# Preamble reordered, fc2's bias added by transfers, the last chunks' fc2 cut in pieces (one Trainium2 core)

## The chip, the cores and the metric

The kernel runs on one core of one Trainium2 chip. The metric is device microseconds (us) of one execution. In the profile the engines are PE (TensorE, matmuls; PEld its weight loads), DVE (VectorE), ACT (ScalarE), POOL (GpSimd) and SP (SyncE, which only issues transfers here).

## The reference

Two layers follow each other on x of 2 sequences x 2048 steps x 256 features, all in float32 (`s` is a sigmoid):

```
xn = layernorm(x)                        # no scale, no shift
i, f, o, z = split(xn @ W + b)           # W is 256 x 1024
i = 10*tanh((i + input_bias)/10);  f = -softplus(f);  o = s(o);  z = tanh(z)
step:  m' = max(f + m, i);  c' = exp(f+m-m')*c + exp(i-m')*z
       n' = exp(f+m-m')*n + exp(i-m');      h = o * c' / (n' + 1e-6)
x = x + h / rms(h) * scale
g = layernorm(x) * gamma + beta
y = silu(g @ w1 + b1)                    # w1 = (fc1_q - 128) * fc1_scales, 256 x 1024
x = x + 0.5 * (y @ w2 + b2)              # w2 = (fc2_q - 128) * fc2_scales, 1024 x 256
```

## The kernel before

The 4096 rows are cut into 8 chunks of 512 steps, taken in turn from the two sequences; chunk c follows chunk c-2 in its sequence. Features lie on the 128 partitions for the gates, the recurrence and fc1, time lies on them for the norms and for fc2's result, so each chunk is turned three times on PE: x after the first norm (`x_turned`), h (`h_turned`), and g after the second norm (`g_turned`). Every matrix product is done on split numbers: a high part in fp32r and the rest as a low part, three matmuls for one (hi*hi, hi*lo, lo*hi). So every activation (xt, gt, y) has an ACT copy to its `_hi` and a DVE subtraction to its `_lo`. The recurrence is three scans on DVE (maximum, denominators, numerators), and the division is exp(-ln(n)) on ACT (`reciprocal`) with a Newton step on DVE (`newton`, `refined`).

The kernel is written engine by engine: each engine has its own program, in an order written out by hand, and semaphores tie them together. An engine takes its instructions strictly in that order, so one that waits holds up all that are behind it. From chunk 4 on a loop over t puts in one turn: gates of chunk t, fc2 of chunk t-3, turns of g(t-2), x(t+1) and h(t-1), and fc1 of chunk t-2. After t = 6 the last chunks are written out.

PSUM holds four banks `mm_ps` (gates and fc1), two banks `z_ps` (fc2's sums, half u of a chunk in one bank, tile n = 2u or 2u+1 in half a bank) and two banks `t_ps` (turns). `fc2(c, tiles)` makes tile n of chunk c from 24 matmuls (8 blocks k of y, three passes each), `fc2_both(c, half)` makes the tiles 0 and 2 (half 0) or 1 and 3 (half 1) side by side, block by block, as y arrives. `final(c, u)` on DVE adds half of fc2's sums to the rows and frees the bank for chunk c+1; SP then stores the rows.

What the change touches by name: `base(c)` on POOL turns the rows into what x + layernorm(x) needs with the small scale (four instructions of 128x256); `base_bias(c)` on DVE adds half of b2 to them; `rms_root`, `ln1_root`, `ln2_root` on POOL are the powers -1/2; `ln1_sums`, `ln1_means` and `ln2_sums`, `ln2` on DVE are the statistics; `g_normalised` is on ACT or POOL by chunk; `silu` on ACT makes y and y_hi, `silu_alone` y only, and then DVE makes y_hi (`y_high`) before y_lo (`y_low`). fc1's two scale groups are folded as a `unit` for the bias and activation, a `ratio` that scales w1's second half, and a `share` that is 1 or 0 and scales its first; `spread` turns such a column into rows on PE with 8 transposes.

## Time and profile before

| what | value |
|---|---|
| time, median of 3 runs | 310.02 us (309.99 to 310.45) |
| the profiled execution's own time | 311.77 us |
| its span, first to last instruction | 310.0 us |
| PE busy, matmuls and weight loads | 294.7 us (95%), 256.3 us (83%) |
| DVE, ACT, POOL busy | 269.5 (87%), 229.7 (74%), 126.4 us (41%) |
| mean granted clock of TensorE | 0.988 of full |
| moved by DMA | 14.73 MB, mean 48 GB/s |

A matmul's row in the timeline has its start, its modelled duration and its operands; matmuls overlap, so the work rate is read from start to start, not from durations. Text in square brackets is the idle time of that engine just before the instruction, with what ended it.

### The profile page before, as it was taken

Reading aid. Unit: us, or ns where it says so; the run is one execution under the profiler, and the core shown is the slowest. Engines: PE = TensorE matmul, PEld = TensorE weight load, DVE = VectorE, ACT = ScalarE, POOL = GpSimd, SP = SyncE. Lnnn points to the kernel's source line nnn. Section 1 sums busy time; section 2 is a strip of 40 time slices with the busy share of each in tenths; the row PEclk is TensorE's granted clock in tenths of the full one; section 3 lists DMA queues with packets and bytes.
Section 4 is the critical chain, followed back from the end, with each engine's and each line's share of the span. In section 5 each row is a group of like instructions: output and inputs, shape, how many; then the busy total and the mean of one; then the engine's idle time right before and its main releaser. Section 6 shows DMA issues by size and latency. Waiting matters only on the chain.

```text
span 310.0 us, 4767 instructions
## 1 busy us (share of the span) xinstructions
PE 294.7 (95%) x1728; PEld 256.3 (83%) x1728; DVE 269.5 (87%) x487; ACT 229.7 (74%) x370; POOL 126.4 (41%) x131
## 2 busy tenths in 40 slices
PE   7999999979899899999999999999999799988996
PEld 5778789856897789988897889987898699868896
DVE  3998989999899999999999997999999987692741
ACT  2699987889879966899876978599866983921720
POOL 3043058300290529512970179012992198155000
PEclk9999999899999999999999999999999979999999
DMA  7980021060000030012000300020000011000201
...
DMA packets 11127, 14.73 MB, mean 48 GB/s; under 512 B 720, under 2 KB 10208, under 8 KB 10848
## 3 DMA queue, kind: packets, MB, share of 16 engines
...
q0 software_dynamic: 320, 1.58, 2.6%
...
## 4 chain that ended last, share of the span: by engine, by line
PE 39%; DVE 38%; issue 11%; ACT 5%; POOL 5%; DMA 2%; DVEq 0%; POOLq 0%; ACTq 0%
PE z_ps L236 5%; PE z_ps L237 4%; PE z_ps L238 4%; DVE y_lo L854 4%; PE mm_ps L236 4%; PE mm_ps L237 4%; PE mm_ps L238 4%; DVE rec L763 3%; DVE rec L756 3%; DVE rec L778 3%; DVE g L822 3%; DVE bn L835 3%; PE mm_ps L329 2%; PE mm_ps L322 2%; DVE rows L830 2%
## 5 line engine op out<-in xcount | busy, mean ns | idle before, releaser
L236 PE MATMUL z_ps<-w_hi,y_hi 128*128 128x256 f32 x248 | 71.8, 290 | 2.6 <-DVE rows L891 1.9
L237 PE MATMUL z_ps<-w_lo,y_hi 128*128 128x256 f32 x248 | 70.9, 286 | 0.0
L238 PE MATMUL z_ps<-w_hi,y_lo 128*128 128x256 f32 x248 | 70.8, 286 | 0.0
L573 ACT ACTIVATE y<-mm_ps,b_all,unit 128x512 f32<-128x512 f32 x54 | 41.6, 770 | 12.8 <-PE mm_ps L329 12.8
L236 PEld LDWEIGHTS z_ps<-w_hi,y_hi 128*128 128x128 f32 x248 | 47.6, 192 | 3.8 <-DVE rows L891 2.1
L237 PEld LDWEIGHTS z_ps<-w_lo,y_hi 128*128 128x128 f32 x248 | 47.6, 192 | 0.3
L238 PEld LDWEIGHTS z_ps<-w_hi,y_lo 128*128 128x128 f32 x248 | 47.6, 192 | 0.0
L322 PE MATMUL mm_ps<-gt_hi,w_hi 128*128 128x512 f32 x124 | 39.9, 403 | 1.6 <-ACT y L573 1.6
L854 DVE TENSOR_TENSOR y_lo<-y,y_hi 128x512 fp32r<-128x512 f32 x56 | 37.6, 687 | 4.0 <-ACT y_hi L576 3.7
L236 PE MATMUL mm_ps<-xt_hi,wg_hi 128*128 128x512 f32 x96 | 38.4, 400 | 1.1 <-ACT f_gate L505 1.1
L329 PE MATMUL mm_ps<-gt_lo,w_hi 128*128 128x512 f32 x124 | 38.8, 394 | 0.0
L237 PE MATMUL mm_ps<-xt_lo,wg_hi 128*128 128x512 f32 x96 | 37.9, 395 | 0.0
L238 PE MATMUL mm_ps<-xt_hi,wg_lo 128*128 128x512 f32 x96 | 37.8, 394 | 0.0
L576 ACT ACTIVATE y_hi<-y 128x512 fp32r<-128x512 f32 x54 | 34.2, 633 | 1.7
L1183 POOL TENSOR_SCALAR rows<-rows,up,nr 128x256 f32<-128x256 f32 x32 | 35.0, 1107 | 0.8
L1154 POOL TENSOR_TENSOR rrms<-meansq,minus_half 128x4 f32<-128x4 f32 x8 | 8.7, 1082 | 60.2 <-DVE meansq L816 60.2
L1161 POOL TENSOR_TENSOR r<-ve,minus_half 128x4 f32<-128x4 f32 x8 | 10.9, 1358 | 47.7 <-DVE ve L849 47.7
L329 PEld LDWEIGHTS mm_ps<-gt_lo,w_hi 128*128 128x128 f32 x124 | 23.3, 188 | 5.5
L322 PEld LDWEIGHTS mm_ps<-gt_hi,w_hi 128*128 128x128 f32 x124 | 22.2, 189 | 6.5 <-ACT y L573 2.4
L325 PE MATMUL mm_ps<-gt_hi,w_lo 128*128 128x512 f32 x62 | 24.5, 395 | 0.0
L236 PEld LDWEIGHTS mm_ps<-xt_hi,wg_hi 128*128 128x128 f32 x96 | 18.1, 189 | 6.3 <-ACT f_gate L505 1.5
L238 PEld LDWEIGHTS mm_ps<-xt_hi,wg_lo 128*128 128x128 f32 x96 | 18.1, 188 | 4.2
...
## 6 DMA issues: line engine op xcount, KB each, us to landing
...
rows<-x SPq DMA_DIRECT2D x7, 512.0 KB, 6.5
q<-fc_q SPq DMA_DIRECT2D x2, 1024.0 KB, 10.8
wg_raw<-fc_scales SPq DMA_DIRECT2D x1, 1024.0 KB, 7.1
w_lo<-q POOLq DMA_DIRECT2D x1, 1024.0 KB, 7.0
wg_raw<-w_gates SPq DMA_DIRECT2D x1, 512.0 KB, 5.7
wg_raw<-w_gates ACTq DMA_DIRECT2D x1, 512.0 KB, 6.0
w_lo<-q POOLq DMA_DIRECT2D x1, 512.0 KB, 4.6
```

The costliest lines, as they stand in the source:

```text
L236: pe.matmul(dst, wh[w_at], ah[a_at], start=start, stop=False)
L237: pe.matmul(dst, wh[w_at], al[a_at], start=False, stop=False)
L238: return pe.matmul(dst, wl[w_at], ah[a_at], start=False, stop=stop)
L322: pe.matmul(dst, w1_hi[:, k, f], gt_hi[:, k], start=(k == 0), stop=False)
L325: pe.matmul(dst, w1_lo[:, f], gt_hi[:, 1], start=False, stop=False)
L329: ins = pe.matmul(dst, w1_hi[:, k, f], gt_lo[:, k], start=False, stop=(k == KD - 1))
L573: act.activation(y[:, j % YBUFS], fc1_bank(c, j), ACT.Silu, bias=b1_all[:, j:j + 1], scale=unit[:, j:j + 1]).then_inc(silu_done, 1)
L576: act.activation(y_hi[:, j], y[:, j % YBUFS], ACT.Copy).then_inc(y_hi_done, 1)
L756: dve.tensor_tensor_scan(rec[s][:, 0, k], f_gate[:, s, k], rec[s][:, 1, k], carry[:, s, 0, k:k + 1], ALU.mult, ALU.max).then_inc(max_done, 1)
L854: dve.tensor_tensor(y_lo[:, j], y[:, j % YBUFS], y_hi[:, j].bitcast(F32), ALU.subtract).then_inc(y_lo_done, 1)
L1161: pool.tensor_tensor(r2[:, 1], ve2[:, s, 1], minus_half[:], ALU.pow).then_inc(ln2_r, 1)
L1183: pool.tensor_scalar(rows[:, b, n], rows[:, b, n], up2[:, n:n + 1], nr2[:, 0, n:n + 1], ALU.mult, ALU.add).then_inc(base_done, 1)
```

## The change

It has four parts.

1. At the start DVE normalises x of chunk 0 at once; the seven small instructions on fc1's scales stand behind chunk 1's normalisation. PE spreads `ratio` after x_turned(1) and `share` after h_turned(0), both into `z_ps`, and w1's first half is then scaled by DVE straight from there (`share_bc` and its two ACT copies are gone). ACT rounds w1's second half during chunk 2's gates. DVE's statistics of chunk 4 are taken in chunk 1's stage, not in chunk 0's.
2. `base_bias` is gone from DVE. In its place POOL, at the end of `base(c)`, issues a transfer that adds the halved b2 (repeated 4 times per partition) to the rows; `final` waits on it.
3. `final` of chunks 3 to 6 stands elsewhere in DVE's order, most of all final(4, 1), which was behind ln2(6) and is now behind residual(6). In the loop x_low(t+1) and the recurrence's product come ahead of final. POOL does base(5) ahead of ln2_root(6).
4. Chunks 5 and 6: fc2's tile 1 is cut in two, half of it ahead of g_turned(c+1); tile 3 comes later, behind h_turned(7) and part of fc1(6) for chunk 5, behind all of fc1(7) for chunk 6. Chunk 6's split y lies in buffers of its own (the gate weights, xt and a new `y_more`), since chunk 7's y is written meanwhile. ACT makes y_hi of all tiles of chunks 6 and 7, and normalises g(7); ahead of g_normalised(6) it loads a table set, and g_high(6) comes ahead of reciprocal(7).

```diff
@@ PE, the last chunks
-            fc2_both(5, 0)
+            fc2_both(5)
+            fc2(5, [1], range(0, KF // 2))
             g_turned(6)
-            fc2_both(5, 1)
-            fc1(6, range(0, 2))
+            fc2(5, [1], range(KF // 2, KF))
+            fc1(6, range(0, 5))
             h_turned(7)
-            fc1(6, range(2, KF))
-            fc2_both(6, 0)
+            fc1(6, range(5, 6))
+            fc2(5, [3])
+            fc1(6, range(6, KF))
+            fc2_both(6)
+            fc2(6, [1], range(0, KF // 2))
             g_turned(7)
-            fc2_both(6, 1)
+            fc2(6, [1], range(KF // 2, KF))
             fc1(7, range(KF))
+            fc2(6, [3])
             fc2(7, range(TT))
@@ PE, the first chunks
-            pe.wait_ge(ratio_step, 2)
-            spread(ratio, z_bank).then_inc(ratio_spread, 1)
...
-            pe.wait_ge(share_ready, 1)
-            spread(share, lambda u: mm_ps[:, 2 + u]).then_inc(share_spread, 1)
-
             first_two_gates()
-            gates(0, range(2, 5))
+            gates(0, range(2, 6))
             x_turned(1)
-            gates(0, range(5, GJ))
+            pe.wait_ge(ratio_step, 2)
+            spread(ratio).then_inc(ratio_spread, 1)
+            gates(0, range(6, GJ))
...
             h_turned(0)
+            pe.wait_ge(gate_done, at(1, 8, 6))
+            pe.wait_ge(w1_scaled, 1)
+            pe.wait_ge(share_ready, 1)
+            spread(share).then_inc(share_spread, 1)
             gates(2, range(2, GJ))
@@ ACT, the last chunks
             silu(5, range(KF))
+            act.preload_act_table_set("natural_log_exp_and_others")
             g_normalised(6)
-            act.preload_act_table_set("natural_log_exp_and_others")
+            g_high(6)
             reciprocal(7)
-            g_high(6)
             act.preload_act_table_set("silu_and_others")
             silu(6, range(0, 2))
             square_sums(7)
-            silu(6, range(2, 6))
-            silu_alone(6, range(6, KF))
+            silu(6, range(2, KF))
+            g_normalised(7)
             g_high(7)
-            for j in range(0, KF, 2):
-                silu(7, range(j, j + 1))
-                silu_alone(7, range(j + 1, j + 2))
+            silu(7, range(KF))
@@ DVE, the loop, t = 5 and 6 (t = 4 in the same sense)
                     h(t - 1)
-                    base_bias(t - 3)
+                    x_low(t + 1)
+                    input_times_z(t)
                     final(t - 3, 0)
-                    input_times_z(t)
-                    x_low(t + 1)
+                    final(t - 3, 1)
                     maximum(t, range(KD))
@@ POOL
                     pool.tensor_scalar(rows[:, b, n], rows[:, b, n], up2[:, n:n + 1], nr2[:, 0, n:n + 1],
                                        ALU.mult, ALU.add).then_inc(base_done, 1)
 
+                pool.wait_ge(base_done, at(c, 4, 4))
+                pool.wait_ge(b2_halved, 1)
+                pool.dma_start(rows[:, b], b2_bc[:].unsqueeze(1).to_broadcast([P, TT, D]), accum_op=ALU.add
+                               ).then_inc(biased[c % 2], 16)
...
             rms_root(6)
+            base(5)
             ln2_root(6)
-            base(5)
             base(6)
```

What stands in each engine's program at three places on which the prediction rests. The first is DVE in chunk 1's stage, from the mean square of h(1) (`meansq`) to the first scan of chunk 2; `bn`, `mv` are the sums and means of the norms. Before:

```order
L816 TENSOR_SCALAR meansq<-sumsq 128x4
L822 SCALAR_TENSOR_TENSOR g<-t_ps,rrms,scale_bc 128x256 x4
L830 TENSOR_TENSOR rows<-rows,g 128x1024
L835 BN_STATS bn<-rows 128x6 x4
L841 BN_AGGR mv<-bn 128x2 x4
L846 TENSOR_SCALAR ve<-mv 128x4
L848 TENSOR_SCALAR nm<-mv 128x4
L849 TENSOR_SCALAR ve<-mv 128x4
L756 SCALAR_TENSOR_TENSOR rec<-f_gate,carry,rec 128x512 x2
```

The same place in the changed kernel:

```order
L832 TENSOR_SCALAR meansq<-sumsq 128x4
L723 BN_STATS bn<-rows 128x6 x4
L838 SCALAR_TENSOR_TENSOR g<-t_ps,rrms,scale_bc 128x256 x4
L846 TENSOR_TENSOR rows<-rows,g 128x1024
L851 BN_STATS bn<-rows 128x6 x4
L857 BN_AGGR mv<-bn 128x2 x4
L862 TENSOR_SCALAR ve<-mv 128x4
L864 TENSOR_SCALAR nm<-mv 128x4
L865 TENSOR_SCALAR ve<-mv 128x4
L729 BN_AGGR mv<-bn 128x2 x4
L733 TENSOR_SCALAR ve<-mv 128x4
L734 TENSOR_SCALAR nm<-mv 128x4
```

Chunk 4's sums (four BN_STATS) now stand behind `meansq`, and its means (three rows) ahead of chunk 2's first scan.

The second is DVE around ln2 of chunk 6; `y_lo<-y,y_hi` is y_low of chunk 5, `rows<-z_ps,rows` is final of chunk 4. Before, from h_scaled(6):

```order
L822 SCALAR_TENSOR_TENSOR g<-t_ps,rrms,scale_bc 128x256 x4
L854 TENSOR_TENSOR y_lo<-y,y_hi 128x512
L830 TENSOR_TENSOR rows<-rows,g 128x1024
L854 TENSOR_TENSOR y_lo<-y,y_hi 128x512 x2
L835 BN_STATS bn<-rows 128x6 x4
L854 TENSOR_TENSOR y_lo<-y,y_hi 128x512
L841 BN_AGGR mv<-bn 128x2 x4
L846 TENSOR_SCALAR ve<-mv 128x4
L848 TENSOR_SCALAR nm<-mv 128x4
L849 TENSOR_SCALAR ve<-mv 128x4
L891 SCALAR_TENSOR_TENSOR rows<-z_ps,rows 128x512
```

In the changed kernel:

```order
L838 SCALAR_TENSOR_TENSOR g<-t_ps,rrms,scale_bc 128x256 x4
L888 SCALAR_TENSOR_TENSOR rows<-z_ps,rows 128x512
L870 TENSOR_TENSOR y_lo<-y,y_hi 128x512 x2
L846 TENSOR_TENSOR rows<-rows,g 128x1024
L888 SCALAR_TENSOR_TENSOR rows<-z_ps,rows 128x512
L870 TENSOR_TENSOR y_lo<-y,y_hi 128x512
L851 BN_STATS bn<-rows 128x6 x4
L870 TENSOR_TENSOR y_lo<-y,y_hi 128x512
L857 BN_AGGR mv<-bn 128x2 x4
```

Both halves of final(4) now stand between h_scaled(6) and ln2's sums; the second was behind all of ln2(6).

The third is POOL from rms_root(6) (`rrms`) on; `r<-ve` with `nr` is ln2_root, `r<-ve` with `nr` and `up` is the start of base. Before:

```order
L1154 TENSOR_TENSOR rrms<-meansq,minus_half 128x4
L1161 TENSOR_TENSOR r<-ve,minus_half 128x4
L1163 TENSOR_TENSOR nr<-nm,r 128x4
L1176 TENSOR_TENSOR r<-ve,minus_half 128x4
L1178 TENSOR_TENSOR nr<-nm,r 128x4
L1179 TENSOR_SCALAR up<-r 128x4
L1183 TENSOR_SCALAR rows<-rows,up,nr 128x256 x4
```

In the changed kernel:

```order
L1143 TENSOR_TENSOR rrms<-meansq,minus_half 128x4
L1165 TENSOR_TENSOR r<-ve,minus_half 128x4
L1167 TENSOR_TENSOR nr<-nm,r 128x4
L1168 TENSOR_SCALAR up<-r 128x4
L1172 TENSOR_SCALAR rows<-rows,up,nr 128x256 x4
L1177 DMA rows<-b_bc 128x4x256
L1150 TENSOR_TENSOR r<-ve,minus_half 128x4
L1152 TENSOR_TENSOR nr<-nm,r 128x4
```

base(5) and its transfer now stand between rms_root(6) and ln2_root(6).

## Rows read from the trace of the kernel before

**Rows 1.** Timeline of PE at the start: start us, us, engine, line, instruction.

```profile
10.94 0.71 PE L289 MATMUL mm_ps<-xt_hi,wg_hi 128*128 128x512 f32 x2
...
19.08 1.09 PE L374 MATMUL t_ps<-ident,xn 128*128 128x128 f32 x8 [0.62 <-DVE xn L729]
```

**Rows 2.** Timeline of PE around the turns of h(2) and h(4).

```profile
99.74 0.63 PE L329 MATMUL mm_ps<-gt_lo,w_hi 128*128 128x512 f32 x2
101.81 1.16 PE L399 MATMUL t_ps<-ident,rec 128*128 128x128 f32 x8 [1.44 <-DVE xt_lo L735]
...
168.35 1.16 PE L399 MATMUL t_ps<-ident,rec 128*128 128x128 f32 x8 [0.65 <-DVE xt_lo L735]
```

**Rows 3.** Timeline of PE in fc2 of chunk 5.

```profile
244.81 0.28 PE L238 MATMUL z_ps<-w_hi,y_lo 128*128 128x256 f32 x1
247.01 0.39 PE L236 MATMUL z_ps<-w_hi,y_hi 128*128 128x256 f32 x1 [1.91 <-DVE rows L891]
```

**Rows 4.** Timeline of PE in fc2 of chunk 6 and the turn of g(7).

```profile
270.74 0.28 PE L236 MATMUL z_ps<-w_hi,y_hi 128*128 128x256 f32 x1
...
277.24 0.39 PE L236 MATMUL z_ps<-w_hi,y_hi 128*128 128x256 f32 x1 [0.35 <-DVE y_lo L854]
...
277.93 0.28 PE L238 MATMUL z_ps<-w_hi,y_lo 128*128 128x256 f32 x1
279.79 1.09 PE L385 MATMUL t_ps<-ident,g 128*128 128x128 f32 x8 [1.58 <-POOL g L1168]
```

**Rows 5.** Windows: us, busy and instructions of each engine, granted clock (PEclk), DMA.

```profile
53.40:56.80 3.40, 3.40 (x13) 2.92 (x12) 3.37 (x6) 2.32 (x3) 0.11 (x1) 0.51 0.00 0
248.00:251.40 3.40, 3.40 (x18) 3.40 (x18) 3.33 (x6) 3.14 (x5) 3.22 (x5) 0.52 0.22 72
256.00:259.40 3.40, 3.40 (x31) 3.40 (x31) 3.40 (x5) 1.20 (x1) 3.22 (x4) 1.00 0.00 0
```

**Rows 6.** Groups of DVE by line: busy us, mean ns, idle before.

```profile
L877 DVE TENSOR_TENSOR rows<-rows,b_bc 128x1024 f32<-128x1024 f32 x8 | 10.7, 1338 | 0.1
```

**Rows 7.** Timeline of DVE, chunks 1 to 3.

```profile
49.04 0.37 DVE L713 BATCH_NORM_AGGREGATE mv<-bn 128x2 f32<-128x6 f32 x4
...
79.28 1.66 DVE L822 SCALAR_TENSOR_TENSOR g<-t_ps,rrms,scale_bc 128x256 f32<-128x256 f32 x4 [1.16 <-POOL rrms L1154]
...
100.98 1.28 DVE L735 TENSOR_TENSOR xt_lo<-t_ps,xt_hi 128x512 fp32r<-128x512 f32 x2
...
116.71 1.41 DVE L707 BATCH_NORM_STATS2 bn<-rows 128x6 f32<-128x256 f32 x4
...
131.64 1.28 DVE L735 TENSOR_TENSOR xt_lo<-t_ps,xt_hi 128x512 fp32r<-128x512 f32 x2
```

**Rows 8.** Timeline of POOL.

```profile
124.02 4.08 POOL L1183 TENSOR_SCALAR rows<-rows,up,nr 128x256 f32<-128x256 f32 x4
...
237.44 1.04 POOL L1154 TENSOR_TENSOR rrms<-meansq,minus_half 128x4 f32<-128x4 f32 x1 [4.45 <-DVE meansq L816]
246.44 1.01 POOL L1161 TENSOR_TENSOR r<-ve,minus_half 128x4 f32<-128x4 f32 x1 [7.96 <-DVE ve L849]
...
251.25 4.23 POOL L1183 TENSOR_SCALAR rows<-rows,up,nr 128x256 f32<-128x256 f32 x4
...
276.04 3.69 POOL L1168 TENSOR_SCALAR g<-rows,r,nr 128x256 f32<-128x256 f32 x4
```

**Rows 9.** Line L1183 (base): count, ns min/median/max, first and last start.

```profile
L1183 POOL TENSOR_SCALAR rows<-rows,up,nr x32: 552/562/2467, 89.4 to 282.9; 128x256 f32<-128x256 f32 x32
```

**Rows 10.** Timeline of ACT: the normalisation of g(6).

```profile
248.25 2.08 ACT L557 ACTIVATE g<-rows,nr,r 128x256 f32<-128x256 f32 x4 [0.86 <-POOL nr L1163]
```

**Rows 11.** The issue of POOL's accumulating transfers: ns min/median/max.

```profile
L1135 POOL DMA_DIRECT2D w_lo<-q x2: 928/930/933, 43.4 to 61.8; - x2
```

**Rows 12.** The same transfers: KB, us from issue to landing.

```profile
w_lo<-q POOLq DMA_DIRECT2D x1, 1024.0 KB, 7.0
...
w_lo<-q POOLq DMA_DIRECT2D x1, 512.0 KB, 4.6
```

More of the change, by code:

```diff
@@ L160, in xt, with y_high_of, y_low_of @@
             return [y_hi[:, 0:KD], y_lo[:, 0:KD]] if c == 1 else [xt_hi[:], xt_lo[:]]
+        def y_high_of(c, j):
+            if c != CHUNKS - 2:
+                return y_hi[:, j]
+            return (wg_hi if j < 4 else wg_lo)[:, j % 4 // 2, j % 2 * T:j % 2 * T + T]
+        def y_low_of(c, j):
+            if c != CHUNKS - 2:
+                return y_lo[:, j]
+            if j < 4:
+                return (xt_hi if j < 2 else xt_lo)[:, j % 2]
+            return y_more[:, j - 4]
         ident_ready, half_ready, zeros_ready = sem("ident_ready"), sem("half_ready"), sem("zeros_ready")
@@ L330, in fc1, with fc2_block, fc2 @@
                     ins.then_inc(fc1_done, 1)
-            def fc2(c, tiles):
+            def fc2_block(c, n, k):
+                dst, rows_of = fc2_out(c, n), slice(n * P, n * P + P)
+                hi, lo = y_high_of(c, k)[:, rows_of], y_low_of(c, k)[:, rows_of]
+                pe.matmul(dst, hi, w2_hi[:, k], start=(k == 0), stop=False)
+                pe.matmul(dst, hi, w2_lo[:, k], start=False, stop=False)
+                return pe.matmul(dst, lo, w2_hi[:, k], start=False, stop=(k == KF - 1))
+            def fc2(c, tiles, blocks=range(KF)):
                 for n in tiles:
@@ L584, in _ @@
             x_high(0)
-            act.wait_ge(share_spread, 1)
-            for u in range(2):
-                act.activation(share_bc[:, u * T:(u + 1) * T], mm_ps[:, 2 + u], ACT.Copy).then_inc(share_out, 1)
             act.wait_ge(bias_ready, 3)
@@ L594, in _ @@
             gates(0, F_TILES)
+            gates(0, range(4, 6))
             x_high(1)
[L596 to L599 removed]
+            gates(0, range(6, GJ))
             x_normalised(2)
@@ L930, in _ @@
             ln1(1)
-            ln1(2)
+            ln1_sums(2)
             x_normalised(1)
+            dve.wait_ge(s1_in, 16)
+            dve.tensor_tensor(tiny[:], s1[:, 0], s1[:, 0], ALU.mult).then_inc(unit_step, 1)
+            dve.wait_ge(unit_step, 1)
+            dve.tensor_scalar(tiny[:], tiny[:], TINY * TINY, 2.0 * TINY, ALU.is_lt, ALU.mult).then_inc(unit_step, 1)
+            dve.wait_ge(unit_step, 2)
+            dve.tensor_tensor(unit[:], s1[:, 0], tiny[:], ALU.add).then_inc(unit_step, 1)
+            dve.wait_ge(unit_step, 3)
+            dve.reciprocal(per_unit[:], unit[:]).then_inc(ratio_step, 1)
+            dve.wait_ge(ratio_step, 1)
+            dve.tensor_tensor(ratio[:], s1[:, 1], per_unit[:], ALU.mult).then_inc(ratio_step, 1)
+            dve.tensor_tensor(share[:], tiny[:], per_unit[:], ALU.mult).then_inc(unit_step, 1)
+            dve.wait_ge(unit_step, 4)
+            dve.tensor_scalar(share[:], share[:], -1.0, 1.0, ALU.mult, ALU.add).then_inc(share_ready, 1)
+            ln1_means(2)
+            maximum(0, range(KD))
+            x_low(1)
             dve.wait_ge(q1_in, 16)
@@ L1078, in _ @@
             g_low(5)
-            base_bias(4)
             denominators(7, range(KD))
-            final(4, 0)
+            divisor(7)
             mean_square(6)
-            divisor(7)
             y_low(5, range(0, 1))
             h_scaled(6)
-            y_low(5, range(1, 2))
+            final(4, 0)
+            y_low(5, range(1, 3))
             residual(6)
-            y_low(5, range(2, 4))
+            final(4, 1)
+            y_low(5, range(3, 4))
             ln2_sums(6)
@@ L1095, in _ @@
             o_times_c(7)
+            g_low(6)
+            final(5, 0)
             newton(7)
             refined(7)
-            g_low(6)
             h(7)
-            base_bias(5)
-            final(5, 0)
-            final(5, 1)
             y_low(6, range(0, 2))
             mean_square(7)
-            y_low(6, range(2, 3))
             h_scaled(7)
+            final(5, 1)
             residual(7)
-            y_low(6, range(3, 4))
+            y_low(6, range(2, 4))
             ln2_sums(7)
@@ L1111, in _ @@
             ln2(7)
-            y_low(6, range(5, 6))
-            for j in range(6, KF):
-                y_high(6, j)
-                y_low(6, range(j, j + 1))
-            base_bias(6)
+            y_low(6, range(5, KF))
             g_low(7)
             final(6, 0)
+            y_low(7, range(KF))
             final(6, 1)
-            base_bias(7)
-            for j in range(KF):
-                y_split_last(j)
             final(7, 0)
```

108 lines of the change are left out of this document (33 added, 75 removed).

## The prediction

> **What bounds the kernel now.** I read the page first: PE is busy for 294.7 of 310.0 us and DVE for 269.5, so either could be the bound, and a share of busy time doesn't tell which. So I went through PE's timeline and looked at the distance from start to start. Work without waits has fixed steps: 0.233 us from one 512-column matmul to the next, 0.119 us for one of fc2 with 256 columns. At these steps PE runs without a break from about 20 us to the end, but for a few places, and these are all that a new order can win, since PE's own work stays the same (each matmul and turn is still there):
>
> - Start: behind the spread of `ratio` and the turn of x(0) the first gates start at 10.94. Then PE waits for xn(1) until 19.08 [rows 1].
> - The turn of h(2) starts 2.07 us after the last pair of fc1 before it, where the step is 0.46: 1.6 us lost, to x_low(4) on DVE. The turn of h(4) waits in the same way for 0.65 us, some 0.8 lost with the restart [rows 2].
> - fc2 of chunk 5 stops after three matmuls: 2.20 us from start to start, for final(4, 1) [rows 3].
> - fc2_both(6, 0) takes 7.19 us from its first start to its last for 48 matmuls, where 47 steps of 0.119 are 5.6: 1.6 lost in small waits for y_lo(6). Then the turn of g(7) waits for POOL: 1.86 from start to start, 1.7 lost [rows 4].
> - Twice the granted clock falls to half (1.2 of 2.4 GHz): from 53.4, behind the 32 one-column matmuls of `shifted_bias`, and from 248.0, right behind the stop at 244.8. In 3.4 us there 18 matmuls of fc2 run, in 3.4 us at full clock 31: 13 x 3.4/31 = 1.4 us lost each time [rows 5].
> - Around 65 to 78 us three more waits, some 3.5 us together, hang on ACT's table loads and the first silus. No part of the change shortens that chain.
>
> **The change, term by term** (minus is gained; times are those of before where nothing else is said).
>
> Start. With the seven scale instructions out of the way DVE normalises x(0) some 0.9 us earlier, and wg_lo, x_low(0) and the gates follow. A sixth gate tile fills the wait for xn(1). I walked DVE, ACT and PE on to the turn of h(0): it can start some 1.1 us earlier. Then the share's 8 transposes come, which cost PE 0.9 and before lay ahead of the first gates. Net -0.15, and -0.15 is also what is left after x_turned(3), as DVE, 2 us ahead by then, waits for that turn anyway.
>
> Chunk 4's statistics. They move from a stretch in which DVE has slack in the new order (it would wait for x_turned(3)) into one that has none: from 79.28 DVE runs densely up to x_low(4), for which PE waits at 101.81. The sums (four of 0.41, 1.4 us as a block) fill DVE's wait of 1.16 us for rms_root(1) [rows 7], and cost next to nothing beyond the 0.15 gained. The means cost 0.37 plus two small rows, 0.6 in all [rows 7]. So x_low(4), which started at 100.98, comes 0.6 later while PE arrives 0.15 earlier: +0.75 on the turn of h(2). Behind DVE there stands ACT's square sum and so on, all late by the same, but not PE-bound.
>
> The clock there. PE then stands 2.8 us from start to start. Two such gaps of before left the clock alone (2.07 and 1.86), one of 2.20 was followed by half clock [rows 2 to 5]. Beyond the longest seen I take the row nearest to it, the 2.20: +1.4. The bounds are 0 and 1.4. What the Trainium skill says on it (TensorE: Matmul & The Clock Gate, Part 4: PE-mode transpose) is that transposes don't count as PE work for the gate; the gap here is followed by 8 transposes, so by the page a fall is more likely than by the length of the gap alone, with the same price. The turn at 101.81 was one of this kind and had none behind it.
>
> b2 by transfer. Eight instructions of mean 1.34 us leave DVE, 10.7 us [rows 6]. I count them at nothing directly: from the turn of h(2) on PE is the bound, and DVE's freed time turns into waits for x_turned. What it does is to remove one stop: x_low(6) now runs ahead of base_bias, product and final, and ends before PE reaches the turn of h(4): -0.8 [rows 2].
> The wait that comes in is final's on the transfer. Rows of before show two of POOL's accumulating transfers, 4.6 us for 512 KB and 7.0 for 1024 [rows 12]; this one is 512 KB in four pieces per partition instead of one, so I take 5 to 7. The tightest place is chunk 1: its base ends at 128.1 [rows 8], the new final(1, 0) stands right behind x_low(5), which ends at 132.9 [rows 7] (and later in the new kernel, with PE's shift). A wait of up to 1 or 2 us there falls into DVE's freed time. Elsewhere (chunks 2 to 6) I find 7 us and more from base's end to final's turn. POOL issues it in 0.93 us [rows 11], with rms_root behind it, ahead of which POOL sat idle for 4.45 us in chunk 6 [rows 8]. Cost 0.
> By the Trainium skill (DMA: Bandwidth & Descriptors, Anatomy of one DMA) such a transfer takes 2.0 us plus its bytes over 436 GB/s, 3.2 us for 512 KB. The row says 4.6, so the measurement goes.
>
> final(4, 1) ahead of ln2(6). DVE finishes it near 243.9 instead of 246.9, ahead of PE's 244.9: -2.1, and with the stop I take away the half clock behind it, -1.4 [rows 3, 5].
>
> The tail. Walked through with durations of before: fc2_both(5) ends at 250.3, half of tile 1 at 251.7. DVE's ln2(6) ends at 247.1 (0.7 later than before, as final(4) now stands ahead), POOL's root at 248.7, ACT is through with y(5) at 247.4, 0.86 ahead of 248.25 [rows 10] and the table at 248.7, g(6) at 250.8: the turn of g(6) doesn't wait. fc1(6, 0) starts at 254.1 instead of 260.6. ACT: g_high(6) to 253.6, reciprocal(7) to 255.7, table to 257.0, silu(6, 0). DVE: h(7) at 259.3; PE gets there at 260.0 after five tiles of fc1(6). Tile 3 of chunk 5 (2.9 us) then covers ACT's silus. The y_lo(6, 5) comes at 271.2 where PE wants it at 270.7: +0.5. ln2(7) ends at 270.6, root at 272.3, and ACT's 2.1 us [rows 10] instead of POOL's 3.7 [rows 8] give g(7) at 274.4, when PE is at 274.9 thanks to the half tile ahead. Of the 1.6 + 1.7 lost before 0.5 stays: -2.85. fc2(6)'s tile 3 behind fc1(7) moves work only; it gives ACT time for y_hi(7) (by its starts in chunk 5 a silu with its copy comes every 1.34 us, a tile of fc1 every 1.17), and y_lo(7, 7) is there 2 us early. The end (last fc2, final, store) is unchanged.
>
> Sum: -0.15 + 0.75 + 1.4 - 0.8 - 2.1 - 1.4 - 2.85 = -5.1 us. The profiled execution took 311.77 with its 310.0 of span, 1.75 above the median; I take the difference from the median: 310.02 - 5.1 = **304.9 us**.
>
> **The rivals.**
>
> *The clock stays up at 100 us* (25%). The windows say that 2.07 didn't suffice and 2.20 once did, so nothing is certain at 2.8. The sum is then 1.4 lower: 303.5. If also the half clock behind shifted_bias falls partly into the tiny matmuls, where it costs nothing, or DVE's chain before 100 us is shorter than walked, up to 1.4 more: 302.1 (8%).
>
> *POOL gets in the way of the tail* (18%). base(5) and its transfer now stand ahead of ln2_root(6). POOL was idle for 7.96 us there, from 238.5 to 246.4 [rows 8]. base needs some 2 us of small ones and 4.2 us for its four big ones [rows 8], then 0.9 to issue: 7.2 us, so it ends near 245.7 and has 1.3 us to spare. But one of the 32 such instructions took 2.47 us where the median is 0.56 [rows 9]; two or three like that in a row add what is spared and 2 us more. Then ln2_root(6) is 1.5 to 2 us late, g(6) as well, and h(7), y(6) and g(7) behind it: 306.5 to 307.5.
> The Trainium skill (SBUF: State Buffer, Who interferes with whom) has a rule for it: a DVE instruction with two SBUF inputs and a POOL one that reads SBUF block each other in full. The trace agrees: four take 4.08 and 4.23 us where 4 x 0.56 would be 2.2 [rows 8, 9].
>
> *The transfers land late: slower than before* (5%). Every final waits for `biased` in DVE's order, and y_low, mean_square and h_scaled stand behind it. If POOL's writing of the transfer's pieces or the accumulation itself took long, say 12 us from base's end to landing, chunks 1 to 4 would hold DVE up by 5 to 7 us each, less the 1.2 freed and about 2 of slack: 2 to 4 us each on PE, 8 to 14 against 5.1 gained, some 315. It decides from about 10 us of landing on. The 7.0 us for twice the bytes [rows 12] speaks against it, the fourfold number of pieces for it.
>
> *The gain is eaten* (4%): another stop takes the place of that of final(4, 1), in which DVE waits for the transfer of chunk 4, and the clock falls with it. Then only the tail is left, and a part of that: 309 to 310.5.
>
> **The numbers.** Likeliest (40%): 304.9, its own range 304.2 to 305.8. With the rivals: 302.1 to 303.5 (33%), 306.5 to 307.5 (18%), 309 and more (9%). The range 302.3 to 307.5 leaves out the last and half of the lowest. Faster by over 0.2% (0.6 us, about what can be told from no change here): 0.93; within it 0.02; slower 0.05.
>
> **What would show it.** In the new profile: first gates near 10.0; a gap before the turn of h(2) of 2.5 to 3 us, with half clock right behind it; none before the turn of h(4); no stop in fc2(5) and full clock there; DVE idle before x_low(5), (6), (7) and not before final; PE without a gap before the turns of g(6), h(7), g(7) but for half a microsecond in fc2(6). I am wrong if DVE shows waits for a transfer at final, or if ACT, not PE, paces chunk 6's silus.

## The result, and the profile after

| | before | after |
|---|---|---|
| median of 5 runs | 310.02 us (309.78 to 311.15) | 307.27 us (306.31 to 308.28) |
| profiled execution | 311.77 us, span 310.0, clock 0.988 | 308.28 us, span 306.5, clock 0.983 |
| DVE busy | 269.5 us | 258.2 us |

The ratio is 0.9907, 95% interval 0.9878 to 0.9936 (2.0 to 3.8 us): 2.75 us gained between medians, 3.5 us between the profiled executions, where 5.1 were forecast. It is faster, inside the range (302.3 to 307.5), and outside the likeliest case's own range (304.2 to 305.8). It lies where the prediction had put the rival on POOL (306.5 to 307.5), and that rival's mechanism didn't come, as is shown below.

PE's timeline of the changed kernel at the places that stand before in [rows 1 to 4]: the first gates, the turns of h(2) and h(4), fc2 of chunk 5, and the turn of g(7).

```profile
9.93 0.73 PE L302 MATMUL mm_ps<-xt_hi,wg_hi 128*128 128x512 f32 x2 [0.58 <-ACT xt_hi L560]
...
99.98 0.63 PE L342 MATMUL mm_ps<-gt_lo,w_hi 128*128 128x512 f32 x2
102.57 1.25 PE L414 MATMUL t_ps<-ident,rec 128*128 128x128 f32 x8 [1.97 <-DVE xt_lo L751]
...
169.83 1.03 PE L414 MATMUL t_ps<-ident,rec 128*128 128x128 f32 x8
...
245.88 0.28 PE L348 MATMUL z_ps<-w_hi,y_hi 128*128 128x256 f32 x1
...
246.12 0.28 PE L350 MATMUL z_ps<-w_hi,y_lo 128*128 128x256 f32 x1
246.96 0.38 PE L348 MATMUL z_ps<-w_hi,y_hi 128*128 128x256 f32 x1 [0.56 <-DVE rows L888]
...
250.91 0.39 PE L348 MATMUL z_ps<-w_hi,y_hi 128*128 128x256 f32 x1 [0.25 <-DVE y_lo L870]
...
277.72 1.03 PE L400 MATMUL t_ps<-ident,g 128*128 128x128 f32 x8
```

Against the rows of before: the first gates come 1.0 earlier, the turn of h(2) 0.76 later, with its wait grown from 1.44 to 1.97. The wait before the turn of h(4) is gone, and so is that before the turn of g(7). But the stop in fc2(5) is still there: 0.84 us from start to start (246.12 to 246.96) where it was 2.20, and a smaller wait for y_lo(5) stands behind it, which wasn't there before.

Windows of the changed kernel (columns as in [rows 5]): half clock behind the one-column matmuls, ahead of fc1(0), and again behind the turn of h(2), and none behind the stop.

```profile
52.30:59.10 6.80, 6.80 (x25) 5.93 (x25) 6.77 (x9) 3.40 (x5) 0.00 (x0) 0.50 0.00 0
103.50:106.90 3.40, 3.40 (x11) 2.72 (x9) 2.83 (x5) 2.18 (x10) 1.96 (x2) 0.50 0.00 0
248.00:251.40 3.40, 3.15 (x25) 2.77 (x24) 3.37 (x15) 2.51 (x3) 1.88 (x2) 1.00 0.88 175
```

The first stretch at half clock is 6.8 us long in this execution, where that of before was 3.4. The gates of chunk 4 start at 108.62 instead of 106.29: 2.33 later, of which 0.76 is the turn's delay and 1.57 the clock.

What makes the stop is seen on DVE. Timeline of DVE in the turn t = 5 of the changed kernel, and the end of final(4, 1) in chunk 6:

```profile
165.27 1.21 DVE L828 TENSOR_TENSOR rec<-rec 128x1024 f32<-128x1024 f32 x1
167.96 1.29 DVE L751 TENSOR_TENSOR xt_lo<-t_ps,xt_hi 128x512 fp32r<-128x512 f32 x2 [1.48 <-ACT xt_hi L560]
169.16 1.21 DVE L805 TENSOR_TENSOR rec<-rec 128x1024 f32<-128x1024 f32 x1
170.30 1.28 DVE L888 SCALAR_TENSOR_TENSOR rows<-z_ps,rows 128x512 f32<-128x512 f32 x2
171.50 2.45 DVE L772 TENSOR_TENSOR_SCAN rec<-f_gate,carry,rec 128x512 f32<-128x512 f32 x2
...
176.74 1.66 DVE L838 SCALAR_TENSOR_TENSOR g<-t_ps,rrms,scale_bc 128x256 f32<-128x256 f32 x4 [0.94 <-POOL rrms L1143]
...
246.23 0.68 DVE L888 SCALAR_TENSOR_TENSOR rows<-z_ps,rows 128x512 f32<-128x512 f32 x1
```

DVE stands idle for 1.48 us before x_low(6), then does the product and both halves of final(2) ahead of the scan, and is idle again for 0.94 before h_scaled. The last row is final(4, 1): it ends at 246.9, where I had put 243.9. POOL, whose base(5) I had taken for the greatest risk, isn't in the way:

```profile
243.03 4.15 POOL L1172 TENSOR_SCALAR rows<-rows,up,nr 128x256 f32<-128x256 f32 x4
247.48 1.35 POOL L1177 DMA_DIRECT2D rows<-b_bc  x1 [0.30 <-POOL rows L1172]
250.35 1.40 POOL L1150 TENSOR_TENSOR r<-ve,minus_half 128x4 f32<-128x4 f32 x1 [1.52 <-DVE ve L865]
```

base(5) takes 4.15 us and its transfer 1.35 to issue, and ln2_root(6) (last row) then still waits 1.52 us for DVE's ln2. The page has the eight transfers with their KB and us from issue to landing:

```profile
rows<-b_bc POOLq DMA_DIRECT2D x8, 512.0 KB, 5.1
```

### The profile page after: what moved, and what is told of

Its sections match the earlier page's. It is cut to its first block, busy times and chain, and to the rows that moved or that the text cites. A ratio compares the mean times of both kernels' runs of the same rounds, so it can differ in the third digit from the quotient of the medians.

```text
span 306.5 us, 4765 instructions
## 1 busy us (share of the span) xinstructions
PE 295.6 (96%) x1728; PEld 257.2 (84%) x1728; DVE 258.2 (84%) x473; ACT 234.8 (77%) x378; POOL 134.7 (44%) x135
## 4 chain that ended last, share of the span: by engine, by line
PE 32%; DVE 29%; POOL 22%; issue 14%; ACT 2%; DMA 1%; POOLq 0%; DVEq 0%
POOL rows L1172 6%; POOL g L1157 4%; DVE y_lo L870 4%; PE mm_ps L253 4%; PE mm_ps L252 4%; PE mm_ps L251 4%; PE z_ps L348 3%; PE z_ps L349 3%; PE z_ps L350 3%; DVE g L838 3%; DVE bn L851 3%; POOL r L1165 3%; DVE rows L846 2%; PE mm_ps L335 2%; PE mm_ps L342 2%
## 5 line engine op out<-in xcount | busy, mean ns | idle before, releaser
L348 PE MATMUL z_ps<-w_hi,y_hi 128*128 128x256 f32 x216 | 61.8, 286 | 0.8 <-DVE rows L888 0.6
L350 PE MATMUL z_ps<-w_hi,y_lo 128*128 128x256 f32 x216 | 61.0, 283 | 0.0
L349 PE MATMUL z_ps<-w_lo,y_hi 128*128 128x256 f32 x216 | 61.0, 283 | 0.0
L594 ACT ACTIVATE y<-mm_ps,b_all,unit 128x512 f32<-128x512 f32 x60 | 46.1, 768 | 5.2 <-PE mm_ps L342 4.5
L870 DVE TENSOR_TENSOR y_lo<-y,y_hi 128x512 fp32r<-128x512 f32 x56 | 38.8, 708 | 7.9 <-ACT y_hi L597 7.8
L348 PEld LDWEIGHTS z_ps<-w_hi,y_hi 128*128 128x128 f32 x216 | 40.8, 189 | 1.7 <-DVE rows L888 0.8
L349 PEld LDWEIGHTS z_ps<-w_lo,y_hi 128*128 128x128 f32 x216 | 40.8, 189 | 0.3
L350 PEld LDWEIGHTS z_ps<-w_hi,y_lo 128*128 128x128 f32 x216 | 40.8, 189 | 0.0
L597 ACT ACTIVATE y_hi<-y 128x512 fp32r<-128x512 f32 x52 | 32.9, 632 | 1.6
L1150 POOL TENSOR_TENSOR r<-ve,minus_half 128x4 f32<-128x4 f32 x8 | 10.3, 1294 | 42.0 <-DVE ve L865 42.0
L1131 POOL TENSOR_TENSOR r<-ve,minus_half 128x4 f32<-128x4 f32 x8 | 11.8, 1474 | 29.8 <-DVE nm L734 29.8
```

The costliest lines, as they stand in the source:

```text
L348: pe.matmul(dst, hi, w2_hi[:, k], start=(k == 0), stop=False)
L349: pe.matmul(dst, hi, w2_lo[:, k], start=False, stop=False)
L350: return pe.matmul(dst, lo, w2_hi[:, k], start=False, stop=(k == KF - 1))
L594: act.activation(y[:, j % YBUFS], fc1_bank(c, j), ACT.Silu, bias=b1_all[:, j:j + 1], scale=unit[:, j:j + 1]).then_inc(silu_done, 1)
L597: act.activation(y_high_of(c, j), y[:, j % YBUFS], ACT.Copy).then_inc(y_hi_done, 1)
L870: dve.tensor_tensor(y_low_of(c, j), y[:, j % YBUFS], y_high_of(c, j).bitcast(F32), ALU.subtract).then_inc(y_lo_done, 1)
```

## The experiments

Twelve kernels, in three groups of four (in the table's order); each group was timed beside the kernel before, whose medians there were 311.21, 310.16 and 311.13 us. So I compare ratios, with the medians beside them where the two differ, and the trace where one execution shows a place.

| kernel | median us | ratio to before, 95% |
|---|---|---|
| changed kernel | 307.27 | 0.9907 (0.9878 to 0.9936) |
| loop_back | 307.96 | 0.9936 (0.9909 to 0.9963) |
| stats_back | 305.92 | 0.9844 (0.9814 to 0.9874) |
| bias_dve | 309.82 | 0.9986 (0.9960 to 1.0013) |
| final_early | 309.35 | 0.9948 (0.9925 to 0.9971) |
| loop_new | 305.56 | 0.9852 (0.9819 to 0.9886) |
| loop_new_stats | 304.79 | 0.9822 (0.9790 to 0.9855) |
| g7_pool | 307.50 | 0.9909 (0.9878 to 0.9939) |
| base5_back | 314.44 | 1.0123 (1.0088 to 1.0158) |
| uncut | 308.13 | 0.9927 (0.9902 to 0.9953) |
| new_bias_dve | 306.11 | 0.9862 (0.9830 to 0.9895) |
| turn_early | 303.84 | 0.9785 (0.9749 to 0.9821) |
| turn_early2 | 305.44 | 0.9843 (0.9810 to 0.9875) |

### loop_back: DVE's order in the loop as before

```diff
@@ DVE, the loop, t = 5 and 6
-                    x_low(t + 1)
-                    input_times_z(t)
                     final(t - 3, 0)
-                    final(t - 3, 1)
+                    input_times_z(t)
+                    x_low(t + 1)
                     maximum(t, range(KD))
                     y_low(t - 2, range(0, 2))
                 mean_square(t - 1)
-                if t == 4:
-                    final(t - 3, 1)
+                final(t - 3, 1)
```

> Changed kernel, but for t = 5 and 6 of the loop DVE's order is that of before (final(t-3, 0) ahead of the product and of x_low(t+1), final(t-3, 1) behind mean_square(t-1)); the transfer for b2 stays. Theory: what kept 0.75 of 2.1 us of the stop in fc2(5), and 0.6 of the 1.4 of clock, is that DVE runs some 3 us later than before in PE's frame from t = 5 on, since x_low, now first, waits for x_turned, the finals stand ahead of the maximum, and nothing fills the wait for rms_root. Then g_low(5) starts 2 to 3 us earlier than the 234.6 of the changed kernel, final(4, 1) ends before PE wants the bank, the stop is gone, and the time is 1.0 to 1.5 us below that of the changed kernel (305.8 to 306.3), if the turn of h(4) doesn't wait again; with up to 0.8 us of wait there, 306.5. Rival: DVE is late because its instructions are slowed by the transfers or by POOL, or because of the wait for rms_root alone; then the order is worth nothing, and the time stays at 307.3.

Measured: not faster than the changed kernel (the intervals overlap, the median is 0.7 higher), where 1.0 to 1.5 us less was expected, although the stop in fc2(5) is gone. From the turn of h(6) to that of g(6) it takes 17.46 us (236.86 to 254.32) instead of 18.89 (235.68 to 254.57). What ate it stands in DVE's timeline, with POOL's and PE's below:

```profile
168.33 0.69 DVE L888 SCALAR_TENSOR_TENSOR rows<-z_ps,rows 128x512 f32<-128x512 f32 x1 [3.51 <-DMA rows<-b_bc]
...
170.07 1.28 DVE L751 TENSOR_TENSOR xt_lo<-t_ps,xt_hi 128x512 fp32r<-128x512 f32 x2
```

```profile
156.80 6.00 POOL L1170 TENSOR_SCALAR rows<-rows,up,nr 128x256 f32<-128x256 f32 x4
163.10 1.35 POOL L1175 DMA_DIRECT2D rows<-b_bc  x1 [0.30 <-POOL rows L1170]
```

```profile
170.90 1.16 PE L414 MATMUL t_ps<-ident,rec 128*128 128x128 f32 x8 [2.56 <-DVE xt_lo L751]
```

final(2, 0) waits 3.51 us for b2's transfer, issued at 163.10 and landed 5.2 later, and x_low(6) stands behind it, for which the turn of h(4) waits 2.56. So x_low ahead of the finals is what makes the transfer harmless: the two parts of the change belong together. The theory is borne out only in part. g_low(5) starts at 234.18, 0.4 us ahead of the changed kernel's 234.60 and not 2 to 3, and PE itself arrives 1.2 us later (the turn of h(6) at 236.86 instead of 235.68). So most of DVE's lead over PE, by which the stop went away, is PE's own delay at the turn of h(4). The cleaner test is loop_new, below.

### stats_back: chunk 4's statistics in chunk 0's stage again

```diff
             ln1(3)
             mean_square(0)
+            ln1_sums(4)
...
             ln2(0)
+            ln1_means(4)
             x_low(3)
...
             mean_square(1)
-            ln1_sums(4)
             h_scaled(1)
             residual(1)
             ln2_sums(1)
             ln2(1)
-            ln1_means(4)
@@ POOL
             ln2_root(0)
+            ln1_root(4)
...
             ln2_root(1)
-            ln1_root(4)
```

> Changed kernel, but chunk 4's sums, means and ln1_root(4) stand in chunk 0's stage again, as before. Theory: the move cost 0.75 us at the turn of h(2) and half clock behind it, 1.57 us as measured by the starts of PE; with the statistics put back the gap before that turn is 2.1 us from start to start, no half clock follows, and PE is 2.0 to 2.3 us earlier from there on. At the end that is 1.5 to 2.3 us off (305.0 to 305.8), less if DVE, which is late in the loop, can't follow. Rival: the statistics only move the delay: in chunk 0's stage they cost the same 0.6 to 2 us before the gates of chunk 2 or at the turn of h(1), and the time stays at 307.3; or the clock falls somewhere else, and half of the gain is left (306.3).

Measured: 0.9844 against 0.9907, some 1.9 us less than the changed kernel by the ratio and 1.35 by the medians, where the theory had 1.5 to 2.3; its slowest run (306.17) is below the changed kernel's fastest (306.31). The wait for x_low(4) at the turn of h(2) is 1.39 us instead of 1.97, the turn is at 101.92 instead of 102.57, and the window behind it is at full clock:

```profile
103.50:106.90 3.40, 3.40 (x17) 2.74 (x16) 2.31 (x6) 3.34 (x11) 1.42 (x1) 1.00 0.00 0
```

Nothing came back in chunk 0's stage: the turn of h(1) is at 70.41 where it was 70.48.

### bias_dve: b2 added by DVE again

```diff
@@ POOL, base(c)
-                pool.dma_start(rows[:, b], b2_bc[:].unsqueeze(1).to_broadcast([P, TT, D]), accum_op=ALU.add
-                               ).then_inc(biased[c % 2], 16)
@@ DVE, the loop, t = 5 and 6
                     h(t - 1)
+                    base_bias(t - 3)
                     x_low(t + 1)
```

> Changed kernel with b2 added by DVE again (eight instructions of 1.34 us, each just ahead of x_low(t+1) or behind g_low), no transfer for it. Theory: the transfers took 10.7 us off DVE, of which most turned into waits; since DVE is 3 us late in the loop anyway, its 1.34 us come back on PE at the turn of h(4) (0.8) and at the stop in fc2(5) (0.7 to 1.5), with the clock behind it: 1.5 to 3.5 us more than the changed kernel, 309 to 311. Rival: the transfers themselves (their issue of 1.35 us on POOL, their traffic) are what makes DVE late; then the time is the same or lower, 306 to 307.3.

Measured: 0.9986, 2.5 us more than the changed kernel by the medians, inside the theory's span. The stop in fc2(5) is 2.15 us long again, with half clock behind it; the turn of h(4) didn't wait, though 0.8 was expected there.

### final_early: the kernel before, final(4, 1) ahead of ln2(6)

```diff
             residual(6)
+            final(4, 1)
             y_low(5, range(2, 4))
             ln2_sums(6)
             y_low(5, range(4, 5))
             ln2(6)
-            final(4, 1)
```

> Kernel before, with one edit: final(4, 1) stands behind residual(6), not behind ln2(6). Theory: in the order of before DVE is early enough, so that this alone takes the whole stop (2.1 us) and the half clock behind it (1.4 us) away; what is behind is late by final's 0.64 us at ln2(6), so ACT's g(6) and with it g's turn are 0.6 us later. Sum 2.2 to 3.5 us less than before: 306.5 to 307.8. Rival: the stop was covered in part by what waits behind it (y_low(5), ln2(6), silu(6)), so that its gain is given back at the turn of g(6): 309 to 310.

Measured: 0.9948, 1.6 us less than before by the ratio, under the 2.2 to 3.5 of the theory. In the profiled execution stop and half clock are both gone, and the turn of g(6) waits 0.55 us for ACT, as foreseen: this turn comes 16.66 us after that of h(6) (234.23 to 250.89) where it was 19.62 (234.38 to 254.00), 3 us less, and nothing is given back at the turn of g(6), as the rival would have it. The median gains less than the profiled execution (3.1 us): four of the twelve runs have a mean clock of 0.983 and take 310.1 to 310.4 us, where the profiled one has 0.993 and 308.63. By the trace the order of before was early enough for the whole term at the stop.

### loop_new and loop_new_stats: the idle places of DVE filled

```diff
@@ DVE, the loop, t = 5 and 6
-                    x_low(t + 1)
                     input_times_z(t)
-                    final(t - 3, 0)
-                    final(t - 3, 1)
+                    x_low(t + 1)
                     maximum(t, range(KD))
                     y_low(t - 2, range(0, 2))
                 mean_square(t - 1)
-                if t == 4:
-                    final(t - 3, 1)
+                final(t - 3, 1 if t == 4 else 0)
                 y_low(t - 2, range(2, 3))
                 h_scaled(t - 1)
+                if t > 4:
+                    final(t - 3, 1)
@@ chunk 6
+            final(4, 0)
             h_scaled(6)
-            final(4, 0)
```

loop_new_stats is this with stats_back's edit.

> Changed kernel, but in the loop (t = 5, 6) DVE takes the product ahead of x_low(t+1), so that it fills the wait for x_turned (1.48 us at 167.96), and both finals stand behind mean_square and h_scaled, where they fill the wait for rms_root (0.94 us); final(4, 0) stands ahead of h_scaled(6) for the same reason. Theory: DVE's lateness in the changed order is this idle time plus the finals ahead of the maximum; x_low(6) still ends in time for the turn of h(4), no final waits for its transfer (the one that waited in the kernel with the loop of before did so because it stood 2 us earlier), final(4, 1) ends 0.6 us or more earlier in PE's frame and the stop in fc2(5) (0.56 us of wait, 0.7 lost) and the wait for y_lo(5) (0.25) are gone: 0.7 to 1.2 us below the changed kernel, a ratio to before of 0.987 to 0.989. Rival: DVE's lateness at fc2(5) comes from the recurrence of chunk 6 alone, behind which the loop's idle time is absorbed (DVE waits 2.38 us for ACT's reciprocal in between); then only final(4, 0) counts, 0.3 to 0.6 us.

> The new loop order together with chunk 4's statistics in chunk 0's stage. Theory: the two are independent, since one acts at the turn of h(2) and the other at fc2(5): the ratio to before is that with the statistics put back alone (0.9844) less 0.7 to 1.2 us, 0.9805 to 0.982. Rival: DVE has no more slack to give, and the stop in fc2(5) comes back at the turn of g(6): 0.984.

Measured: 0.9852 and 0.9822. loop_new is 1.7 us below the changed kernel, more than the 0.7 to 1.2 expected; the intervals just touch, but at the same mean clock the runs lie apart (at 0.994 305.05 to 305.91 against 306.31 to 307.27, at 0.983 306.7 against 308.1 and 308.3). The two edits together reach 2.6, less than the 3.6 of the parts, which the intervals (0.3% each) leave room for. DVE's timeline in loop_new:

```profile
166.16 1.21 DVE L805 TENSOR_TENSOR rec<-rec 128x1024 f32<-128x1024 f32 x1
167.78 1.29 DVE L751 TENSOR_TENSOR xt_lo<-t_ps,xt_hi 128x512 fp32r<-128x512 f32 x2 [0.41 <-ACT xt_hi L560]
...
174.89 1.65 DVE L838 SCALAR_TENSOR_TENSOR g<-t_ps,rrms,scale_bc 128x256 f32<-128x256 f32 x4
...
240.20 0.69 DVE L888 SCALAR_TENSOR_TENSOR rows<-z_ps,rows 128x512 f32<-128x512 f32 x1 [0.43 <-DMA rows<-b_bc]
...
244.71 0.68 DVE L888 SCALAR_TENSOR_TENSOR rows<-z_ps,rows 128x512 f32<-128x512 f32 x1
```

The idle 1.48 is down to 0.41, the 0.94 before h_scaled is gone, and final(4, 1) ends at 245.4, before PE wants the bank at 245.9. final(4, 0) waits 0.43 us for its transfer, which the expectation had ruled out. PE has neither the stop nor the wait for y_lo(5) left: from the first start of fc2(5) to the last matmul it takes 56.42 us (245.56 to 301.98) where the changed kernel takes 57.69, 1.27 less. So it was the order, not the transfers' traffic, since all eight transfers are still there. The edit also moves final(4, 0), but DVE's lead is there ahead of it: the mean square of h(6) starts at 238.53 instead of 239.80, 1.27 of the 1.52 us by which final(4, 1) comes earlier. The rival, that the loop's idle time is absorbed before chunk 6, is thereby out.

### g7_pool and uncut: what took away the wait before the turn of g(7)

g7_pool gives g(7)'s normalisation back to POOL, uncut puts tile 1 of fc2(6) whole behind the turn:

```diff
@@ ACT and POOL, g7_pool
             silu(6, range(2, KF))
-            g_normalised(7)
             g_high(7)
...
             ln2_root(7)
+            g_normalised(7)
             base(7)
@@ PE, uncut
             fc2_both(6)
-            fc2(6, [1], range(0, KF // 2))
             g_turned(7)
-            fc2(6, [1], range(KF // 2, KF))
+            fc2(6, [1])
```

> Changed kernel with g(7) normalised by POOL again. Theory: in the tail ACT's 2.08 us in place of POOL's 3.7 is part of what took away the wait before the turn of g(7). In the changed kernel g(7) ends 0.36 us ahead of its turn; with 1.6 us more PE waits 1.3 us there, and base(7) is later too, which costs nothing as it has time until the last final: 1.2 to 1.4 us more than the changed kernel. Rival: the half tile of fc2 ahead of the turn was enough for that, and the normalisation's engine gives 0 to 0.4 us.

> Changed kernel, but tile 1 of fc2(6) stands whole behind the turn of g(7). Theory: with g(7) by POOL the time stayed the same, because POOL took 2.17 us for it in the tail, not the 3.7 of before; so what took away the wait before the turn of g(7) is the half tile ahead of it (12 matmuls, 1.4 us), with the 0.36 us by which g(7) is early: PE waits 1.1 us there, and the time is 1.1 us above the changed kernel. Rival: fc2_both(6), which runs without small waits now, gained it all, as all of PE's chain behind h(7) moved: then 0 to 0.3 us.

Measured: 0.9909, no difference, so the theory on g7_pool fell; and 0.9927 for uncut, about 0.6 us more than the changed kernel, with intervals that overlap. The first has its reason in POOL's timeline:

```profile
274.34 2.17 POOL L1156 TENSOR_SCALAR g<-rows,r,nr 128x256 f32<-128x256 f32 x4
```

2.17 us, where the row of before has 3.69 for the same four instructions [rows 8], and ACT 2.08. And in uncut PE waits where the theory has it:

```profile
275.94 0.28 PE L350 MATMUL z_ps<-w_hi,y_more 128*128 128x256 f32 x1
277.19 1.09 PE L400 MATMUL t_ps<-ident,g 128*128 128x128 f32 x8 [0.96 <-ACT g L577]
```

By the trace that is 1.25 us from start to start, against 0.12. At this turn the half tile does it, and the engine of g(7) nothing; what it is worth in the time (0.6 us by the ratio, 0.9 by the medians, 1.1 expected) stays imprecise.

### base5_back: base(5) behind ln2_root(6) on POOL

```diff
             rms_root(6)
-            base(5)
             ln2_root(6)
+            base(5)
             base(6)
```

> Changed kernel with base(5) behind ln2_root(6) on POOL again. Rival of the prediction (POOL in the way of ln2_root(6)): then the root would come earlier and 1 to 2 us would be gained. Theory: POOL waited 1.52 us for DVE's ln2 in front of that root, so the order is worth nothing to it: the same time as the changed kernel within 0.3 us; and base(5) with its transfer, 7 us later, still lands ahead of final(5, 0).

Measured: 1.0123, some 6.7 us more than the changed kernel; both expectations missed. DVE and PE in this kernel:

```profile
261.25 0.69 DVE L888 SCALAR_TENSOR_TENSOR rows<-z_ps,rows 128x512 f32<-128x512 f32 x1 [6.16 <-DMA rows<-b_bc]
```

```profile
265.65 1.97 PE L414 MATMUL t_ps<-ident,rec 128*128 128x128 f32 x8 [5.07 <-DVE rec L828]
```

```profile
252.47 3.24 POOL L1172 TENSOR_SCALAR rows<-rows,up,nr 128x256 f32<-128x256 f32 x4
256.01 1.35 POOL L1177 DMA_DIRECT2D rows<-b_bc  x1 [0.30 <-POOL rows L1172]
```

The transfer, issued at 256.01, lands at 261.2. final(5, 0) waits 6.16 us for it, and newton(7), refined(7) and h(7) stand behind it on DVE, so PE waits 5.07 at the turn of h(7). I had looked at whether POOL's root comes earlier and not at what stands behind final(5, 0). It is the mechanism of the rival "the transfers land late", though here the landing takes 5.2 us as elsewhere and it is the issue that comes late: a final that waits takes the recurrence with it. Half clock follows on this wait. base(5) ahead of the root keeps that away.

### new_bias_dve: b2 on DVE in the new order

The edit is bias_dve's, on top of loop_new_stats, but in the loop:

```diff
                 mean_square(t - 1)
+                if t > 4:
+                    base_bias(t - 3)
                 final(t - 3, 1 if t == 4 else 0)
```

> The new loop order and the statistics put back, but b2 added by DVE (at the turn of chunks 2 and 3 behind mean_square, where DVE waits for rms_root). Theory: in a good order too the transfers are worth time, since 1.34 us each delays h_scaled, ln2 and the recurrence; at fc2(5) DVE is then 1.2 us late again (base_bias(4) stands ahead of the denominators), and the stop comes back: 1.0 to 2.4 us more than the same order with transfers (304.8), 305.8 to 307.2. Rival: the order alone does it, and DVE's waits hide the eight instructions: 304.8 to 305.3.

Measured: 0.9862, 1.2 us more than loop_new_stats by the ratio, as the theory has it; the intervals overlap, but the runs don't (305.44 to 306.45 against 304.56 to 305.05). The stop in fc2(5) is back at 1.21 us. So the transfers seem to be worth about half as much in this order as in that of the change (2.5).

### turn_early and turn_early2: y_low behind x_low(4)

```diff
@@ DVE, chunk 2's stage, turn_early2 (turn_early leaves y_low(1, 0) where it is)
-            y_low(1, range(0, 1))
             h(2)
-            y_low(1, range(1, 2))
             x_low(4)
-            y_low(1, range(2, 3))
+            y_low(1, range(0, 3))
```

> The new loop order and the statistics put back, and y_low(1, 1) behind x_low(4) instead of ahead of it. Theory: the turn of h(2) waits 1.44 us for x_low(4), and DVE runs densely in front of it, so each instruction taken from its front counts in full: 0.6 us less (304.2). Rival: y_low(1, 1) is late for ACT's buffers or fc2(1), nothing gained (304.8).

> As the one before, with y_low(1, 0) behind x_low(4) as well. Theory: 1.2 us less than with neither moved (303.6), of which ACT may take back 0.2, as its fifth silu waits for the buffer of y(1, 0). Rival: the silus and the square sums of h(2) behind them are late by the same 1.2 us, and h_scaled(2) with them: 304.2 to 304.8.

Measured: 0.9785 for turn_early, the fastest of all: 303.84 us, 3.4 below the changed kernel and 0.95 below loop_new_stats by the medians, where 0.6 was expected (the intervals overlap, the runs don't). The wait at the turn of h(2) is 0.78 us where loop_new_stats had 1.44. turn_early2 brings it to 0.31 and is slower all the same (0.9843, 305.44 us), beyond what theory and rival had:

```profile
102.95 0.78 ACT L594 ACTIVATE y<-mm_ps,b_all,unit 128x512 f32<-128x512 f32 x1 [1.34 <-PE mm_ps L342]
```

```profile
111.90 0.50 PE L251 MATMUL mm_ps<-xt_hi,wg_hi 128*128 128x512 f32 x1 [0.88 <-ACT rec L524]
```

ACT's fifth silu of chunk 1 needs the buffer that y_low(1, 0) frees. It stands idle 1.34 us, not the 0.2 of my expectation, and chunk 4's gates wait 0.88 for ACT later (the row puts the silu's wait down to PE, which had long been done there). The next turn, of h(3), then has a gap of 0.61 us from start to start where 0.23 is its step.

## Why the prediction was right, and where it was off

Measured by starts of PE in the two profiled executions (after minus before), by the prediction's own terms:

| term | forecast | measured |
|---|---|---|
| start and chunk 4's statistics, turn of h(2) | +0.60 | +0.76 |
| half clock behind it | +1.4 | +1.57 |
| turn of h(4) | -0.8 | -0.85 |
| stop in fc2(5) | -2.1 | -1.36 |
| half clock behind the stop | -1.4 | -1.4, gone as forecast |
| new waits for y_lo(5) | 0 | +0.55 |
| tail | -2.85 | -2.64 |
| elsewhere, ahead of fc2(5) | 0 | -0.18 |
| sum | -5.1 | -3.5 |

The tail's two places are fc2_both(6), 6.29 us from its first start to its last instead of 7.19, and the turn of g(7), 0.12 us behind the matmul before it instead of 1.86. fc2_both(6) so keeps 0.7 us of waits for y_lo(6), where the prediction left 0.5.

The direction and most of the terms are right by their mechanism. That the median is inside the range is in part luck: it owes this to the upper bound, which was set for POOL's rival, and that rival didn't come.

**The failed step** is "DVE finishes it near 243.9 instead of 246.9, ahead of PE's 244.9". final(4, 1) ended at 246.9 as before. I had taken DVE's freed 10.7 us for slack and let its times of before stand; but from t = 5 on it ran some 3 us later than before while PE was 1.3 to 1.5 later (h_scaled(4) starts at 176.74 where it was 173.59; the turn of h(6) at 235.68 where it was 234.38), since x_low in front waits for x_turned, both finals stand ahead of the scan, and nothing fills the wait for the root. loop_new shows it by taking that away: stop and wait for y_lo(5) gone, 1.27 us. Another 0.2 lies in y_low(5) itself, two of which take 1.49 us at 243.67, beside POOL's base(5), where two take 1.28 at 242.54 before. The failed step cost 0.74 at the stop and 0.55 behind it, 1.3 of the 1.6 us between forecast and measurement.

**Statistics and clock.** Right: +0.76, and in the profiled execution the clock fell. stats_back took both back. But the clock there isn't settled by the wait. Seven profiled kernels had a wait of 1.92 to 2.12 us before this turn; half clock followed in four (changed kernel, loop_new, g7_pool, uncut) and not in three (loop_back, bias_dve, base5_back). None of the others, with 1.44 or less, had it. In the changed kernel's five runs the mean clock was 0.994 three times (306.31 to 307.27 us) and 0.983 twice (308.08 and 308.28). The profiled execution has 0.983, with half clock for 6.8 us at 52 and for 3.4 behind the turn; 0.994 leaves room for one stretch of 3.4 us, and the record doesn't say at which place: loop_back's profiled execution, at 0.994, has it at 52 us, g7_pool's, at 0.994 too, behind the turn of h(2). So whether "the clock stays up" (25%) came true in some of the runs is open. The median lies in the group with less half clock, and the forecast took one fall for certain.

**The Trainium skill on transposes** (TensorE: Matmul & The Clock Gate, Part 4: PE-mode transpose): the fall behind the turn of h(2) fits what it says, that transposes don't count as busy in the same way, but the three kernels in which eight transposes followed the same wait at full clock show that it doesn't decide.

**b2 by transfer.** Landing in 5.1 us and no wait at final: right. "Elsewhere I find 7 us and more from base's end to final's turn" was wrong for chunk 2, where base ends at 164.45 and final(2, 0) starts at 170.30: 5.85 us, with 0.30 and 5.1 of them for issue and landing, 0.4 to spare. loop_back and base5_back show the price when it isn't there, 2.6 and 5.1 us at PE. Issue took 1.35 us, not 0.93.

**The rival on POOL** (18%) didn't come: nothing stretched base(5) beyond 4.15 us, and POOL had 1.52 us to spare, where the prediction counted 1.3. Both came some 3 us later than forecast. With DVE earlier, in loop_new, POOL still waits 1.53 us for it.

**The start.** The first gates came at 9.93 as forecast. But half clock at 52 us lasted twice as long and took fc1(0) from 58.31 to 59.80; the waits on ACT behind it swallowed all but 0.17 by the turn of h(1), 0.32 more than the -0.15 forecast. In stats_back the profiled execution (306.07, clock 0.989) has this long stretch; the runs at 0.989 took 305.86 to 306.17 and those at 0.994 305.72 and 305.82. If it is the long stretch that tells them apart, which only the profiled one shows, it costs little.

**Profile and median.** The profiled execution of before lay 1.75 above its median and that of after 1.0. The runs of before show why: in the first group five of 29 have a clock of 0.999 and lie at 308.87 to 310.29, and of the 20 with 0.988 or 0.989 most lie near 311.3. So the half clock behind the stop, of which the prediction took 1.4 us away, isn't there in every run of before. By a difference of two profiled executions the change is worth 3.5, by medians 2.75.
